# The image attention's inverse sums turned in the side bank, one unit earlier, and multiplied one step later

## The reference, cut to what matters

```
x = layer_norm(image_embeds);  l = layer_norm(latents)
q = l @ Wq;  k, v = split(concat([x, l], 1) @ Wkv)          # 16 heads of 64
w = softmax((q * scale) @ (k * scale)^T)                      # 512 x 666 for each head and batch
out = (w @ v) as [B, 512, 1024] @ Wo
```

## Time and profile before

| what | value |
|---|---|
| median of 3 runs | 2154.32 us (2142.14 to 2154.53) |
| profiled execution | 2150.68 us |
| its span | 2148.9 us |
| first and last row maximum of the image attention | 35.9 and 783.4 us from the span's start |
| busy in that stretch of 747.5 us | PE 658.80, DVE 529.68, ACT 485.63, POOL 445.70 |
| granted clock of TensorE there | 0.97 of full |

### The profile page before, as it was taken

One profiled execution on the slowest core, in us unless ns is written; L12 is line 12 of the kernel. 1 busy time (PEld: TensorE's weight loads), 2 busy tenths in 40 slices (PEclk: granted clock), 3 DMA queues, 4 the chain that ended last, 5 costly groups with the idle time before them and its releaser, 6 DMA issues.

```text
span 2148.9 us, 34188 instructions
## 1 busy us (share of the span) xinstructions
PE 1728.8 (80%) x12709; PEld 1075.3 (50%) x12848; DVE 1321.8 (62%) x3131; ACT 966.7 (45%) x2073; POOL 599.1 (28%) x723
## 2 busy tenths in 40 slices
PE   4899889988988987999623978996985886579997
PEld 2566656665666655776413644552444333424444
DVE  6777677767767744776487575655457455643333
ACT  4677557756766744997100633553321443201111
POOL 3567567656545540000000224200001200200000
PEclk9999989998999997999665788998997787789998
DMA  5000000000000001001000000000000000000000
GB/s 206 14 14 21 14 14 14 20 14 14 14 14 17 17 9 72 2 2 69 6 0 0 1 8 5 1 2 1 1 1 1 1 1 1 0 0 0 6 5 10
DMA packets 14598, 33.01 MB, mean 15 GB/s; under 512 B 3594, under 2 KB 9058, under 8 KB 13538
## 3 DMA queue, kind: packets, MB, share of 16 engines
q1 hardware_dynamic: 14433, 30.81, 4.6%
HBM read 18.84 MB, written 1.05 MB: 9 GB/s over the span
## 4 chain that ended last, share of the span: by engine, by line
PE 56%; DVE 27%; issue 7%; ACT 7%; POOL 2%; DMA 0%; ACTq 0%; DVEq 0%; POOLq 0%
PE banks L449 14%; DVE work L692 4%; PE banks L649 4%; PE banks L665 3%; PE banks L2288 3%; PE banks L1672 3%; PE banks L638 3%; PE banks L2284 3%; DVE xn L395 2%; DVE work L710 2%; ACT work L790 2%; PE banks L593 2%; PE banks L1655 1%; PE banks L424 1%; PE banks L2336 1%
## 5 line engine op out<-in xcount | busy, mean ns | idle before, releaser
L903 POOL TENSOR_TENSOR work<-work 128x512 bf16<-128x512 f32 (+1 forms) x448 | 374.1, 862 | 79.5 <-ACT work L805 75.7
L790 ACT ACTIVATE work<-banks,work 128x666 f32<-128x666 f32 x256 | 208.5, 814 | 251.3 <-DVE work L692 172.3
L649 PE MATMUL banks<-const,work 128*128 128x128 f32 (+1 forms) x1536 | 234.8, 285 | 51.1 <-ACT work L805 45.2
L389 POOL TENSOR_TENSOR norm_room<-norm_room,minus_half 128x4 f32<-128x4 f32 x48 | 50.0, 1041 | 757.1 <-DVE norm_room L384 757.1
L692 DVE TENSOR_REDUCE work<-banks 128x1 f32<-128x666 f32 x256 | 215.8, 843 | 63.7 <-PE banks L638 63.1
L649 PEld LDWEIGHTS banks<-const,work 128*128 128x128 f32 (+1 forms) x1536 | 158.3, 136 | 101.9 <-ACT work L790 53.2
L449 PE MATMUL banks<-work,weights_b 128*128 128x512 bf16 x823 | 192.6, 389 | 16.2 <-DVE work L1996 5.6
L665 PE MATMUL banks<-work 128*64 128x256 bf16 (+1 forms) x2304 | 177.7, 283 | 11.6 <-POOL work L903 10.5
L638 PE MATMUL banks<-work 128*128 128x154 bf16 (+1 forms) x980 | 182.7, 308 | 3.1 <-ACT work L790 0.4
L805 ACT ACTIVATE work<-banks 128x512 f32<-128x512 f32 x256 | 150.7, 589 | 3.3 <-PE banks L649 3.3
L424 PE MATMUL banks<-const,xn 128*128 128x128 f32 x176 | 40.2, 370 | 129.5 <-DVE xn L395 80.9
(11 more groups left out here) (348 smaller groups left out, 3268.2 us busy)
## 6 DMA issues: line engine op xcount, KB each, us to landing
work<-work SPq DMA_DIRECT2D x64, 166.5 KB, 2.7
weights_b<-in_weights SPq DMA_DIRECT2D x1, 4116.0 KB, 23.1
weights_b<-in_weights SPq DMA_DIRECT2D x1, 2824.0 KB, 9.9
weights_a<-in_weights SPq DMA_DIRECT2D x1, 2056.0 KB, 10.6
weights_a<-in_weights SPq DMA_DIRECT2D x1, 2050.0 KB, 10.0
rows<-in_rows SPq DMA_DIRECT2D x1, 1496.0 KB, 13.1
weights_c<-in_weights SPq DMA_DIRECT2D x1, 1288.0 KB, 5.8
weights_b<-in_weights SPq DMA_DIRECT2D x1, 1027.5 KB, 12.0
```

Of the source, the lines that this page charges most:

```text
L649: m = pe.transpose(ps[0:rows, c:c + P], prob[:, t * P:t * P + rows], self.eye)
L790: ac.activation(self.probs[i % 4], self.slot[i % 2][:, 0:KEYS0], ACT.Exp, bias=self.neg_max[i % 4], accum_out=self.sums[u % 2][:, 2 * j + ...
L903: po.tensor_tensor(parts[:, :, :, 0], exact, parts[:, :, :, 1], ALU.subtract).then_inc(self.mark(event, i - 3))
```

## The change

The sums and inverses get four places each. A new function `image_spread(i)` names the unit `u = i // 4 - 1`, one later than `back`, that is four steps earlier in the unit's life. At i % 4 = 1 DVE takes the reciprocal and POOL spreads it. At i % 4 = 3 PE turns it into bank 7 (`side`), under the bank's own rule, behind the turning of the exponentials; ACT copies it, behind kept_a, to a place of its own (`spread_t`, two halves of `scratch`). The multiplication on DVE moves from i % 4 = 2 to i % 4 = 3, reads bank 6 and `spread_t`, and, from the second batch on, waits itself for the event `brought` of the projection with Wo that read the old `mixed`; before, ACT's copy had that wait. The projections with Wo and the chores behind them come two steps later, and there is one step more.

```
-        self.sums = [self.place(4) for _ in range(2)]
-        self.inverse = [self.place(4) for _ in range(2)]
+        self.sums = [self.place(4) for _ in range(4)]
+        self.inverse = [self.place(4) for _ in range(4)]
...
+        self.spread_t = [self.scratch[:, 2 * n:2 * n + 2, :].rearrange("p t n -> p (t n)") for n in (0, 1)]
...
-        late = i - 8 * PAIRS - 7
+        late = i - 8 * PAIRS - 9
...
+    def image_spread(self, i):
+
+        u = i // 4 - 1
+        return (u, {1: "invert", 3: "turn"}.get(i % 4)) if 0 <= u < UNITS else (None, None)
...
-                if part == 2:
-                    pe.wait_ge(*self.at("spread", back + 1))
-                    for j in (0, 1):
-                        t = pe.transpose(self.out_bank[:, (2 + j) * P:(3 + j) * P],
-                                         self.spread[back % 2][:, j, :, :].rearrange("p h d -> p (h d)"), self.eye)
-                    t.then_inc(self.mark("spread_turned"))
             if 2 <= i < SUBS + 2:
                 self.image_turn_pe(pe, i - 2)
+            u, what = self.image_spread(i)
+            if what == "turn":
+                self.bank(pe, 7, "spread_kept", u + 1)
+                pe.wait_ge(*self.at("spread", u + 1))
+                for j in (0, 1):
+                    t = pe.transpose(self.side[:, j * P:(j + 1) * P], self.spread[u % 2][:, j, :, :].rearrange("p h d -> p (h d)"), self.eye)
+                t.then_inc(self.mark("spread_turned"))
...
+            if what == "invert":
+                ve.wait_ge(*self.at("exp", 4 * u + 4))
+                if u >= 4:
+                    ve.wait_ge(*self.at("spread", u - 3))
+                ve.reciprocal(self.inverse[u % 4], self.sums[u % 4]).then_inc(self.mark("inverted"))
+            back, b = i // 4 - 2, (i // 4 - 2) // 2 // PAIRS
+            if 0 <= back < UNITS and i % 4 == 3:
                 ve.wait_ge(*self.at("spread_kept", back + 1))
-                ve.tensor_tensor(out, self.out_bank[:, 0:2 * P], out, ALU.mult).then_inc(self.mark("mixed"))
+                ve.wait_ge(*self.at("weighed", back + 1))
+                if b >= 1:
+                    ve.wait_ge(*self.at("brought", QT * (b - 1) + 2 * (back % 2) + 2))
+                ve.tensor_tensor(self.mixed[:, back // 2 % PAIRS, back % 2 * 2 * P:(back % 2 + 1) * 2 * P], self.out_bank[:, 0:2 * P],
+                                 self.spread_t[back % 2], ALU.mult).then_inc(self.mark("mixed"))
...
-                if i % 4 == 0 and u >= 2:
-                    ac.wait_ge(*self.at("inverted", u - 1))
+                if i % 4 == 0 and u >= 4:
+                    ac.wait_ge(*self.at("inverted", u - 3))
...
+            u, what = self.image_spread(i)
+            if what == "turn":
+                ac.wait_ge(*self.at("spread_turned", u + 1))
+                if u >= 2:
+                    ac.wait_ge(*self.at("mixed", u - 1))
+                ac.activation(self.spread_t[u % 2], self.side[:, 0:2 * P], ACT.Copy).then_inc(self.mark("spread_kept"))
```

More of the change, by code:

```diff
@@ L520, in image_chores @@
                 out.append((("once", "once_scale", "again", "again_scale", "columns")[i - first], b))
-        late = i - 8 * PAIRS - 7 - 6
+        late = i - 8 * PAIRS - 9 - 6
         if late >= 0 and late % (8 * PAIRS) in (1, 2, 4) and late // (8 * PAIRS) < BATCH - 1:
@@ L533, in image_steps @@
     def image_steps(self):
-        return range(SUBS + 15)
+        return range(SUBS + 16)
     def image_sub(self, i):
@@ L694, in image_ve @@
                 self.image_lows_ve(ve, (i - 1) // 8 + 1, (i - 1) % 8 // 2)
[L695 to L702, removed]
-                ve.wait_ge(*self.at("spread_kept", back + 1))
-                ve.tensor_tensor(out, self.out_bank[:, 0:2 * P], out, ALU.mult).then_inc(self.mark("mixed"))
+            u, what = self.image_spread(i)
[6 more added lines that the diff above has]
+            if 0 <= back < UNITS and i % 4 == 3:
+                ve.wait_ge(*self.at("spread_kept", back + 1))
+                ve.wait_ge(*self.at("weighed", back + 1))
[3 more added lines that the diff above has]
+                                 self.spread_t[back % 2], ALU.mult).then_inc(self.mark("mixed"))
             if 2 <= i < SUBS + 2:
@@ L786, in image_ac @@
                     ac.wait_ge(*self.at("turned_b", i - 3))
-                if i % 4 == 0 and u >= 2:
-                    ac.wait_ge(*self.at("inverted", u - 1))
+                if i % 4 == 0 and u >= 4:
+                    ac.wait_ge(*self.at("inverted", u - 3))
                 ac.wait_ge(*self.at("max", i + 1))
                 ac.activation(self.probs[i % 4], self.slot[i % 2][:, 0:KEYS0], ACT.Exp, bias=self.neg_max[i % 4],
[L791 to L799, removed]
+                              accum_out=self.sums[u % 4][:, 2 * j + h:2 * j + h + 1]).then_inc(self.mark("exp"))
             if 2 <= i < SUBS + 2:
@@ L877, in image_po @@
         for i in self.image_steps():
[L878 to L884, removed]
+            u, what = self.image_spread(i)
+            if what == "invert":
+                if u >= 2:
+                    po.wait_ge(*self.at("spread_turned", u - 1))
+                po.wait_ge(*self.at("inverted", u + 1))
+                by_head = self.inverse[u % 4].rearrange("p (j h) -> p j h", j=2).unsqueeze(3).to_broadcast([P, 2, 2, D0])
+                po.tensor_copy(self.spread[u % 2], by_head).then_inc(self.mark("spread"))
             for what, b in self.image_chores(i):
```

## The result

| | before | changed |
|---|---|---|
| median | 2154.33 us (2142.14 to 2154.53) | 2175.04 us (2167.39 to 2179.93) |
| profiled execution | 2150.68 us | 2167.39 us |
| its span | 2148.9 us | 2165.6 us |
| first to last row maximum of the image attention | 747.5 us | 761.6 us |
| steady group | 21.25 us | 21.80 us |

The ratio is 1.0107, with a 95% interval from 1.0061 to 1.0153: slower by about 1%, at the edge of what I had called measurable. The forecast was 2166 us, the range 2138 to 2190.

The account below looks back on a forecast made before the run. PE was taken to bound the group (19.62 of 21.25 us busy). Steady groups +8.3, changes of batch +9, first groups +1, end -3.3 sum to +15 on the profiled 2150.68 us: 2166 us, range 2138 to 2190.

Parts of the forecast that it names:

- PE's gaps and the transposes: Steady group: gaps in steps 0, 2, 4 and 6 close, -1.15 us; transposes leave steps 2 and 6, -0.54 us.
- The wait for bank 7: Steps 3 and 7: PE waits for DVE's low parts before turning the inverse, +1.47 and +0.68 us a group.
- no change: Rival: waits in steps 3 and 7 are given back next steps, or block terms are -1; about 2151 us, chance 0.12.
- The steady group: Image attention away from batch changes: +0.46 us a group, to 21.7 us; +8.3 us for 18 groups.
- The changes of batch: Three blocks of four groups where the batch changes: +3 us a block, +9 in all, bounds -1 and +8 a block.
- The two ends: Image attention's two first groups +1 us; last group -2.4 and the path behind the last product -0.9, together -3.3 us.
- The product that overwrites bank 6: Step after the multiplication's new step 3: the product finds the multiplication done, so its move costs nothing.
- no wait for the bank: Lower bound for a steady group: only 0.27 us more in each of steps 3 and 7, -1.15 us a group.
- The faster rival: Bank 7 is free in time in steps 3 and 7: -1.15 us for 27 groups, 2116 us; chance 0.10.
- The clock: Rival: new waits of 1.5 us lower PE's clock in every group, about 1.6 us each, +43, 2209 us; chance 0.09.
- the projections with Wo hold the multiplication: Rival, batch changes: DVE's multiplication waits for the projection's product; three blocks cost 8 us, not 3: 2181 us; chance 0.17.
- my own sign: Test for the projections holding the multiplication: the row maximum of steps 4 and 0 starts after the product's end.

Follow-up runs that it names:

- e6: Changed kernel (inverse still in bank 7) with the multiplication ahead of DVE's low parts and projections with Wo and chores at their old steps: 2205.23 us, ratio 1.0270.
- e3: The kernel before, unchanged, run once more for a second trace: image stretch 742.5 us, steady group 21.24 us.
- e11: The changed kernel, run once more for a second trace: 2172.09 us, ratio 1.0099 to the kernel before.
- e4: Changed kernel, but turning of the inverse and ACT's copy stay in bank 6 at steps 2 and 6, as before: 2158.56 us, ratio 1.0036.
- e1: Changed kernel, but the inverse is turned in the free half of bank 5 at steps 0 and 4: 2162.95 us, ratio 1.0057.
- e2: Kernel before, with only a PE wait for bank 7 added at steps 3 and 7, no instruction moved: 2204.76 us, ratio 1.0252.
- e7: Changed kernel with only the projections with Wo and the chores put back two steps earlier: 2164.63 us, ratio 1.0073.

## Why the prediction was right

**What bounds the group.** PE, and it stayed PE. The 86.1 us before the multiplication fell to 24.5, and all that PE had of it was its own short gaps, as the first part had said.

**PE's gaps and the transposes.** Both long gaps went. From the starts of the scores, steps 0 and 4 are shorter by 0.55 and 0.54 us, steps 2 and 6 by 0.22 and 0.21, steps 1 and 5 as before: -1.52 in all (where the first record of a step's scores is missing, its start is an estimate from the second, 0.22 us back). I had predicted -1.15 for the gaps and -0.54 for the transposes, -1.69.

**The wait for bank 7.** Predicted +1.47 and +0.68, by the chain from the scores over the row maximum and the low parts. Measured idle before the transposes 1.14 and 0.89. Step 3 took some 3.27 us against my 3.30, +1.44, and step 7 2.54 against my 2.58, +0.64. e6 lengthened the chain by 0.34 and the wait grew by as much (1.14 to 1.47, and 0.89 to 1.22 in step 7), which shows DVE's queue up to the low parts as its cause. Nothing of it was given back in the next steps, so the rival "no change" fell.

**The steady group.** Predicted 21.7, measured 21.80: +0.55 instead of +0.46. Over the 18 groups that is +10.0 instead of +8.3.

**The changes of batch.** Predicted +9 in three blocks. The four groups of each took 109.8, 109.7 and 100.1 us before and 111.3, 110.8 and 104.0 after: +6.6. The second traces of the two kernels (e3, e11) give +14.6, so the term can't be told to better than several us. What I had not written down is how it is made up: the first group of a block lost its projection and was 2 us shorter (23.8 to 21.8), and the third got longer (29.5 to 32.5). The last group of the last block is also one of my 18 steady ones, so my sum counts its 0.46 twice.

**The two ends.** The two first groups, predicted +1, gave -0.5 in the first traces and +1.3 in the second ones. For the last group I had put down -2.4, a figure that my own terms (-0.54 and -1.15) do not give; its seven steps between the first and the last row maximum fell from 17.1 to 15.6 us, -1.5. From the last row maximum to the first projection with Wo it took 11.02 us before (783.38 to 794.40) and 10.02 after: -1.0 against -0.9.

**The sum.** +15 predicted for the whole. The image attention gave +14.0 and -1.0, so +13.0 in the first pair of traces. The second pair gives 742.5 to 766.6 us for the image stretch, +24.1; over two traces of each kernel the mean is +19.1, and +18 with the end. The medians are 20.7 apart. So 13 and 15 agree better than the evidence allows, and in part by luck: in this pair the steady groups were put too low by 1.7 and the last group by 0.9, the blocks too high by 2.4 and the first groups by 1.5. Two traces of one kernel differ by 5 us in the image stretch and up to 6 behind it; what of the rest belongs to the change stays open.

**The step that failed: "The product that overwrites bank 6 starts 0.65 us into the next step and finds it done: nothing."** It is true of the changed kernel only, because PE waits for the low parts first. As a reason it was wrong: the multiplication was moved behind 0.84 and 1.40 us of DVE's work, and with bank 7 free the product waits 1.34 and 0.74 us (e4). My bound for "no wait for the bank", -1.15 a group, was too good by all of that: e1 and e4 show +0.1. The faster rival, 2116 us, could not have come about by a free bank alone. I had asked for each wait what is late next, except for the one that I thought removed. In the forecast this cost nothing, because the longer wait covered it.

**The rivals.** The clock did not fall in the steady groups of the changed kernel, but it fell in e2 behind 1.61 us and in part of e6 behind 1.48, so 0.09 was not too much, and the distance was small. The waits of 1.69 and 0.97 us that I set against it are not in one group: the second, at 428.95, lies ahead of the stretch from 431.60. The argument holds for the first, behind which the clock stayed at 1.00 until 459.

The Trainium skill (page "TensorE: Matmul & The Clock Gate", section "HAM oscillation — how this bites in real kernels") describes a loop that falls to the lower level at each of its waits, and those are waits for a DMA of some 3 to 5 us. The waits of e2 and e6 are shorter and the clock fell all the same, and at the 1.14 us of the changed kernel it did not, so "this rival would be the rule" was more than the page says.

That the projections with Wo hold the multiplication came about, in two steps of each block. DVE's idle time has 20.1 us of it (L714 behind L600), and by my own sign the row maximum starts after the product's end (248.57 + 2.02):

```profile
248.57 2.02 PE L600 MATMUL banks<-weights_a,work 128*128 128x128 f32 x16 [0.56 <-ACT scratch L815]
...
250.73 0.42 DVE L714 TENSOR_TENSOR work<-banks,scratch 128x256 f32<-128x256 f32 x1 [3.22 <-PE banks L600]
...
251.66 0.84 DVE L699 TENSOR_REDUCE work<-banks 128x1 f32<-128x666 f32 x1
...
252.11 0.87 PE L656 MATMUL banks<-const,work 128*128 128x128 f32 x6
```

But PE's turning behind it has no idle time, so PE hid most of it: the other such step, a step 0, takes 3.05 us (266.62 to 269.67) against 2.82 in the steady group (345.04 to 347.86). The rival's price of 8 us a block was not paid for this. In e7 L714 waits for L600 no more, and the image stretch is only 1.3 us shorter, though e7 moves other work too.

## What to carry to other kernels

Before moving an instruction to a later step, look at what stands ahead of it on its engine there, and ask who waits for what it frees: here two moves (turning into the busiest bank, multiplying behind the low parts) each reach the same queue on DVE (0.84 + 1.40 us in step 3), and undoing one only uncovers the other. A wait removed from an engine that isn't the bound gains nothing unless the bound's own gaps close; and an instruction that frees a bank belongs ahead of work that nobody waits for, which made the same idea 1.4% faster instead of 1% slower. That holds where the bank is the one that PE waits for: with the inverse in bank 7 the same order cost 2.7% (e6).

## What the runs showed of the hardware

The granted clock can part two groups with the same instructions and the same wait: in e6 a wait of 1.47 us left 1.00 and 22.47 us, one of 1.48 us gave 0.93 and 24.01 us, and the kernel stayed in either kind for two groups and more. Behind 1.14 us (steady groups of the changed kernel) the clock stayed at 1.00, behind 1.61 us (e2) it fell in every steady group. The length of the wait alone does not tell it: behind one of 1.69 us in the kernel before, at 445.05, it stayed at 1.00 from 445 to 459 us. And 6 us of difference in 1370 can come from layers that no edit touched (1365.5 and 1371.9 us in two executions of one kernel).
